# Output and feed-forward matmul chunks spread one by one over all even slots

## What is computed

```python
c_kv, c_q = h @ W_dkv, h @ W_dq                  # rank 128
k, v   = c_kv @ W_uk, c_kv @ W_uv                # 16 heads, 48 and 64 wide
q      = c_q @ W_uq ;  q_rot, k_rot = rotary(c_q @ W_qr), rotary(h @ W_kr)   # 16 wide
attn   = softmax([q, q_rot] @ [k, k_rot].T / 8) @ v
x      = layernorm(h + attn @ W_o)
w      = int4_rounded(W_ffn)
out    = layernorm(x + x @ w + bias + (x @ a) @ b)
```

## Time and profile before

| | us |
|---|---|
| median of 3 runs | 2160.74 (2158.69 to 2166.31) |
| the profiled execution, device time | 2158.53 |
| its span, core 6 (slowest) | 2157.0 |
| spans of the other cores | 2140.2 to 2154.1 |
| ScalarE busy | 2016.5 (93%) |
| TensorE busy | 1938.3 (90%) |
| VectorE busy | 602.7 (28%) |

### The profile page before, as it was taken

How to read it: one execution, slowest core, us unless ns; L and a number is a source line. 1 busy time by engine, 2 the same in 40 slices (tenths; PEclk the granted TensorE clock), 3 DMA queues, 4 the chain that set the end, 5 groups by cost and what they waited for, 6 DMA issues and landing times.

```text
span 2157.0 us, 61016 instructions; the slowest of 8 cores (2140.2 to 2157.0 us)
## 1 busy us (share of the span) xinstructions
PE 1938.3 (90%) x22544; PEld 708.4 (33%) x22544; DVE 602.7 (28%) x1084; ACT 2016.5 (93%) x2177; POOL 256.6 (12%) x303
## 2 busy tenths in 40 slices
PE   5977888989999999998999999999999999999976
PEld 2422333333333333333333333333333333333323
DVE  2731411232223322222222322323222322322224
ACT  2689999989999999998999999999999999999973
POOL 2000000110011110110111100211111100211021
PEclk9999999999999999999999999999999999999998
DMA  9772300121122211221121211312121311323121
GB/s 166 164 148 80 107 23 27 51 92 43 36 83 67 87 45 53 71 71 69 41 93 50 99 36 36 103 54 81 45 92 48 102 31 41 102 85 118 41 70 39
DMA packets 78681, 155.69 MB, mean 72 GB/s; under 512 B 16192, under 2 KB 46912, under 8 KB 78400
## 3 DMA queue, kind: packets, MB, share of 16 engines
q1 hardware_dynamic: 64672, 106.86, 15.5%
q0 software_dynamic: 13728, 44.93, 8.7%
HBM read 109.75 MB, written 40.76 MB: 70 GB/s over the span
## 4 chain that ended last, share of the span: by engine, by line
ACT 69%; issue 16%; PE 6%; DMA 3%; DVE 2%; ACTq 2%; SPq 1%; POOL 0%; DVEq 0%; POOLq 0%
ACT Psb L1004 69%; ACTq L998 2%; DMA wbuf<-hG 1%; DMA rbc<-rec 1%; SPq L495 1%; PE PS L742 1%; PE PS L916 1%; PE PS L858 1%; PE PS L944 1%; DMA osb<-hG 1%; PE PS L729 1%; PE PS L879 1%; PE PS L774 1%; PE PS L769 1%; PE PS L754 1%
## 5 line engine op out<-in xcount | busy, mean ns | idle before, releaser
L1004 ACT ACTIVATE Psb<-PS 128x1024 bf16<-128x1024 f32 x2048 | 1933.9, 1025 | 34.8 <-PE PS L858 22.5
L858 PE MATMUL PS<-Qsb,Ksb 64*128 64x512 bf16 x4096 | 804.0, 387 | 149.4 <-ACT Psb L1004 138.5
L879 PE MATMUL PS<-Psb,Vsb 128*32 128x512 bf16 x8192 | 634.1, 386 | 0.5 <-ACT Psb L1004 0.5
L858 PEld LDWEIGHTS PS<-Qsb,Ksb 64*128 64x128 bf16 x4096 | 212.9, 93 | 702.5 <-issue 696.4
L889 PE MATMUL PS<-Psb,ones_sb 128*32 128x256 bf16 x8192 | 404.1, 274 | 3.5 <-issue 3.5
L889 PEld LDWEIGHTS PS<-Psb,ones_sb 128*32 128x32 bf16 x8192 | 221.7, 97 | 224.2 <-issue 8.1
L1154 DVE TENSOR_TENSOR X<-PS,X 128x512 f32<-128x512 f32 x112 | 77.5, 692 | 625.5 <-PE PS L835 330.0
L879 PEld LDWEIGHTS PS<-Psb,Vsb 128*32 128x32 bf16 x8192 | 127.9, 94 | 236.5 <-issue 236.5
L831 PE MATMUL PS<-wbuf,osb 128*128 128x512 bf16 x448 | 135.6, 384 | 0.0
L802 PE MATMUL PS<-wbuf,osb 128*128 128x512 bf16 x448 | 135.6, 384 | 0.0
L1126 DVE COPY rec<-PS 128x256 f32<-128x256 f32 x64 | 27.1, 423 | 344.9 <-PE PS L889 344.9
(11 more groups left out here) (111 smaller groups left out, 690.8 us busy)
## 6 DMA issues: line engine op xcount, KB each, us to landing
wbuf<-wo_p POOLq DMA_DIRECT2D x32, 512.0 KB, 7.0
rbc<-rec SPq DMA_DIRECT2D x512, 32.0 KB, 1.8
X<-h SPq DMA_DIRECT2D x28, 512.0 KB, 3.9
x_scr<-X SPq DMA_DIRECT2D x28, 512.0 KB, 2.6
X<-x_scr SPq DMA_DIRECT2D x28, 512.0 KB, 3.4
wbuf<-wf_p POOLq DMA_DIRECT2D x28, 512.0 KB, 6.9
out<-X SPq DMA_DIRECT2D x28, 512.0 KB, 2.6
X<-W_ffn SPq DMA_DIRECT2D x16, 512.0 KB, 4.4
```

Of the source, the lines that this page charges most:

```text
L858: m = pe.matmul(PS[:, b0 + 512 * hh:b0 + 512 * (hh + 1)], Ksb[rows, k0:k0 + 128], Qsb[rows, 512 * p:512 * (p + 1)], tile_position=(64 * hh ...
L879: pe.matmul(PS[32 * j:32 * (j + 1), b0:b0 + 512], Vsb[:, v0:v0 + 32], Psb[:, p0 + 512 * (j // 2):p0 + 512 * (j // 2 + 1)], start=first and ...
L1004: act.activation(Psb[:, 1024 * (g % 4):1024 * (g % 4 + 1)], PS[:, 1024 * (g % 2):1024 * (g % 2 + 1)], AF.Exp, scale=0.125).then_inc(sem["e ...
```

## The change

`o` steps become 8 of one chunk and `f` steps 9 (the ninth is the low-rank matmul). The planner gives each `o` chunk 1.4 slots of its time and each `f` chunk 1.47, so an even slot holds one or two chunks of one group; the first chunk of a group begins a slot of its own, and every other step takes one even slot and moves the planner's time by 2. Waits and counts stay tied to the same matmuls. In tiles 1 to 6 the places become: `o` in slots 8 to 104; `qr` at 106 and 108; `qp` 0 to 2 at 112, 114 and 118; `tr` 3 at 116; `z` and `f` in slots 122 to 232 (`z` at 122, 150, 178, 206); `qp` 3 to 6 at 234, 236, 238 and 240. Of the even slots of such a tile 38 then have two chunks (18 `o`, 20 `f`), 60 have one (28 `o`, 32 `f`), and 12 are empty. The end of the last output group stays at slot 104 (chunk 7 alone), the end of the last feed-forward group moves from 244 to 232 (chunks 7 and 8), and with it GpSimd's load of the output weights.

```diff
-                    for i in range(4):
-                        seq.append((8, ("o", qt, sub, half, i)))
+                    for c in range(8):
+                        seq.append((8, ("o", qt, sub, half, c)))
...
-                    for i in range(5):
-                        seq.append((122, ("f", qt, sub, half, i)))
+                    for c in range(9):
+                        seq.append((122, ("f", qt, sub, half, c)))
...
         when = {}
-        t = 0.0
+        t, last = 0.0, -2
         for lo, st in seq:
             t = max(t, lo)
-            when[st] = 2 * int(t / 2 + 0.5)
-            at(T, when[st], st)
-            t += 2.8
+            if st[0] in ("o", "f"):
+
+                slot = max(last if st[-1] else last + 2, 2 * int(t / 2 + 0.5))
+                t += 1.4 if st[0] == "o" else 1.47
+            else:
+                slot = max(last + 2, 2 * int(t / 2 + 0.5))
+                t = slot + 2
+            when[st] = last = slot
+            at(T, slot, st)
...
-            for ph, kind, i in ((1, "o", 3), (2, "f", 4)):
+            for ph, kind, i in ((1, "o", 7), (2, "f", 8)):
...
-                at(T, when["o", qt, 3, 1, i] + 0.1, ("wf", qt, i))
-                at(T, when["f", qt, 3, 1, i] + 0.1, ("wo", qt, i))
+                at(T, when["o", qt, 3, 1, 2 * i + 1] + 0.1, ("wf", qt, i))
+                at(T, when["f", qt, 3, 1, 2 * i + 1] + 0.1, ("wo", qt, i))
```

TensorE's part, for `o` (that for `f` alike):

```diff
-                    sub, half, c2 = st[2:]
-                    if c2 == 0:
+                    sub, half, c = st[2:]
+                    if c == 0:
                         pe.wait_ge(sem["ev_misc"], misc_of(st))
-                    for c in (2 * c2, 2 * c2 + 1):
-                        if sub == 0 and half == 0:
...
-                        m = pe.matmul(bank(7), osb_tok(qt, sub, c),
...
+                    m = pe.matmul(bank(7), osb_tok(qt, sub, c),
...
-                    if c2 == 3:
+                    if c == 7:
                         m.then_inc(sem["mm_misc"], 1)
```

More of the change, by code:

```diff
@@ L361, in build_program @@
         for st in bg_at[g]:
-            if st[0] in ("qr", "qp", "tr", "z") or (st[0], st[-1]) in (("o", 3), ("f", 4)):
+            if st[0] in ("qr", "qp", "tr", "z") or (st[0], st[-1]) in (("o", 7), ("f", 8)):
                 misc_no[st] = n_misc
@@ L366, in misc_of @@
     def misc_of(st):
-        last = {"o": 3, "f": 4}
+        last = {"o": 7, "f": 8}
         return misc_no[st[:4] + (last[st[0]],)] if st[0] in last else misc_no[st]
@@ L669, in tail_step @@
                     else:
-                        gp.wait_ge(sem["mm_misc"], misc_no["f", qt, 3, 1, 4] + 1)
+                        gp.wait_ge(sem["mm_misc"], misc_no["f", qt, 3, 1, 8] + 1)
                     gp.dma_start(out=wbuf[:, 2048 * c:2048 * (c + 1)],
@@ L675, in tail_step @@
                     gp.wait_ge(sem["st_wf"], 128)
-                    gp.wait_ge(sem["mm_misc"], misc_no["o", qt, 3, 1, 3] + 1)
+                    gp.wait_ge(sem["mm_misc"], misc_no["o", qt, 3, 1, 7] + 1)
                     gp.dma_start(out=wbuf[:, 2048 * c:2048 * (c + 1)],
@@ L793, in tail_step @@
                 if st[0] == "o":
-                    sub, half, c2 = st[2:]
-                    if c2 == 0:
+                    sub, half, c = st[2:]
+                    if c == 0:
                         pe.wait_ge(sem["ev_misc"], misc_of(st))
-                    for c in (2 * c2, 2 * c2 + 1):
-                        if sub == 0 and half == 0:
-                            pe.wait_ge(sem["nrm_done"], NP * qt + c + 1)
-                            if c % 2 == 0:
-                                pe.wait_ge(ld_wo[c2], 16 * (qt + 1))
-                        m = pe.matmul(bank(7), osb_tok(qt, sub, c),
-                                      wbuf[:, 1024 * c + 512 * half:1024 * c + 512 * (half + 1)],
-                                      start=(c == 0), stop=(c == 7))
-                    if c2 == 3:
+                    if sub == 0 and half == 0:
+                        pe.wait_ge(sem["nrm_done"], NP * qt + c + 1)
+                        if c % 2 == 0:
+                            pe.wait_ge(ld_wo[c // 2], 16 * (qt + 1))
+                    m = pe.matmul(bank(7), osb_tok(qt, sub, c),
+                                  wbuf[:, 1024 * c + 512 * half:1024 * c + 512 * (half + 1)],
+                                  start=(c == 0), stop=(c == 7))
+                    if c == 7:
                         m.then_inc(sem["mm_misc"], 1)
@@ L824, in tail_step @@
                 if st[0] == "f":
-                    sub, half, c2 = st[2:]
-                    if c2 == 0:
+                    sub, half, c = st[2:]
+                    if c == 0:
                         pe.wait_ge(sem["ev_misc"], misc_of(st))
-                    if sub == 0 and half == 0 and c2 < 4:
-                        pe.wait_ge(ld_wf[c2], 16 * (qt + 1))
-                    for c in range(2 * c2, min(8, 2 * c2 + 2)):
+                    if sub == 0 and half == 0 and c < 8 and c % 2 == 0:
+                        pe.wait_ge(ld_wf[c // 2], 16 * (qt + 1))
+                    if c < 8:
                         pe.matmul(bank(7), osb_tok(qt, sub, c),
@@ L833, in tail_step @@
                                   start=(c == 0), stop=False)
-                    if c2 == 4:
+                    else:
                         pe.matmul(bank(7), zb_sb[:, :], bpad_sb[:, 512 * half:512 * (half + 1)],
@@ L1134, in ep_step @@
                     if qt >= 2 and p == 0:
-                        dve.wait_ge(sem["mm_misc"], misc_no["f", qt - 2, 3, 1, 4] + 1)
+                        dve.wait_ge(sem["mm_misc"], misc_no["f", qt - 2, 3, 1, 8] + 1)
                     dve.tensor_tensor(osb_pair(qt, p), bank(4 + P % 2), rbc[:, :], op=ALU.mult
@@ L1147, in tail_step @@
             def tail_step(st):
-                if (st[0], st[-1]) in (("o", 3), ("f", 4)):
+                if (st[0], st[-1]) in (("o", 7), ("f", 8)):
                     qt, sub, half = st[1:4]
```

## The result

The changed kernel takes 2178.77 us (median of 4 runs, 2178.54 to 2180.61), the kernel before 2160.23 (4 runs, 2158.69 to 2166.31): a ratio of 1.0078 with a 95% interval of 1.0056 to 1.0100, so it is slower, by 17 us. The median lies 0.8 above the upper end of the predicted range, 2178; the ratio times the 2160.74 that the prediction started from gives 2177.6, just inside it. The side and the two mechanisms are those forecast.

A forecast was written before the change was run, and what follows sets the result against it. ScalarE's exponentials on the slowest core were taken to bound the kernel. 2158.5 - 11 + 13 + 6 = 2166.5 us for a profiled execution, plus 2.2 for the runs' median, gave 2168 us, range 2148 to 2178 (forecast's own 2160 to 2175).

The forecast's parts named there:

- the two mechanisms: Weight loads meeting the ends of broadcasts at head pairs 2 and 6, making multiplies late: +6 and +13 us.
- What bounds the kernel: Whole kernel: ScalarE works 93% of 2157.0 us, nearly all on 2048 exponentials; the slowest core sets the time.
- Part 1: Output and feed-forward chunks: fewer heavy even slots save 1.6 us per tile, -11 us over seven tiles (-15 to -9).
- a cadence of 0.940: Sign for the chunk saving: exponentials among chunks come every 0.940 us instead of 0.951.
- Rival C: Added single-chunk visits on TensorE are not hidden and cost 21 us: 2171, up to 2182 us; chance 0.07.
- Part 2: Slots 96 and 104: pair 2's broadcast moves some 0.2 us closer to the feed-forward-weight load; +6 us, tiles 1 to 6.
- The announced sign: Slots 96 to 120 in tiles 4 to 6 take 24.4 us instead of 23.4, showing the pair 2 loss.
- Part 3: Slots 232 to 240: output-weight load meets pair 6's broadcast, its late multiply delays query chunks; +13 us (0 to 18).
- threshold of 3.1 us: Pair 6's multiply may start up to 3.1 us after the output-weight load starts; later delays TensorE's slot 238.
- Part 4: Slot 204: a feed-forward group ends where VectorE's multiply of pair 5 stands ahead of its addition; half a microsecond in all.
- rival D: Pair 2's shortened broadcast-to-load distance costs its upper bound in half the tiles: 15 us, not 6; 2177 to 2185; chance 0.08.
- Rivals A and B: A (0.25): pair 6's multiply in time, pair 2 unmoved, 2149.5 us; B (0.25): only pair 6 pays, 2162.5 us.

The follow-up runs named there:

- e7: Changed kernel, output-weight load held until head pair 6's multiply, one chunk moved from slot 96 to 94 and chunk 6 from 102 to 104: 0.9953 of the kernel before.
- e1: Changed kernel with the output-weight load held back until VectorE's multiply of head pair 6 is done: 1.0001 of the kernel before.
- e9: Changed kernel, output-weight load held until head pair 6's multiply, one output chunk moved from slot 96 to 94; second timing: 1.0001 of the kernel before.
- e5: Changed kernel with only query chunks 3 to 6 moved back, to slots 244 to 250, both weight loads unchanged: 0.9992 of the kernel before.
- e3: Changed kernel with output-weight and feed-forward-weight loads held back until the multiplies of head pairs 6 and 2 respectively: 0.9906 of the kernel before.
- e4: Kernel before with only the feed-forward-weight load held back until head pair 2's multiply is done: 0.9950 of the unedited kernel before.

## Why the prediction was right or wrong

**What bounds the kernel**: right. Wherever time was lost, the exponentials of line 1009 started late; in the kernel after they idle 27.2 us more than before, on slowest cores that differ by 22.1.

**Part 1, the chunks, -11 us**: right. It measured 0.9950 - 0.9906, 9.5 us, and 1 - 0.9953, 10.2 us, for e7, although e7 still stalls 3.1 more than the kernel before (17.7 + 1.7 against 14.1 + 2.2). So the pattern itself is worth 10 to 13; tile 7 says 1.7 x 7 = 12. Announced was a cadence of 0.940; it came to 0.942 beside the output chunks and 0.946 beside the feed-forward chunks. That the added visits are hidden holds too: single-chunk steps take 1.78 and 1.94, 3.72 together. The Trainium skill, TensorEngine Tiling (Array Packing), Key Properties, has TensorE drain at each change of the tiling mode. Paid in full at every added visit, by the price worked out from the rows, that would be 21 us; the trace does not agree as far as the time goes, since a single step ends before the next exponential does. Rival C is out.

**Part 2, slot 96 and slot 104, +6 us**: right in its mechanism, too small by four tenths. The shift of the broadcast was forecast as 0.12 to 0.18 and came to 0.18; the load came only 0.04 earlier, not 0.1. From e1 and e9 to e7 it measured 1.0001 - 0.9953 = 0.0048, 10.4 us. The term that was mis-sized is "I take 1 for each of tiles 1 to 6, nearer the quiet tiles": 6 us in the sum, 10.4 measured by the ratios, known to some 7, and 8 by the stalls of e1 and e7. Tiles 4 to 6 were quiet because the last issue stood 0.16 (odd cores) or 0.06 (even cores) ahead of the load. The earlier trace rows hold two points of that curve, 2.1 on core 7 and 3.5 on core 6, and I called it steep; a shift of 0.2 along it leads to 4.9 and 5.3, which is 2.5 per tile on an odd core and 2.0 on an even one, twice what I took. Tiles 1 to 3, which I had as lost already, lost more as well: their stall is 5.2 to 5.8 instead of 2.8 to 4.2. An instruction packet is beside all 24 of these meetings in both kernels, but the last issue is late (8.8 or more after slot 96) in 6 of them before and in 15 after, so part of this loss may not be the shift's. The announced sign, 24.4 for slots 96 to 120 in tiles 4 to 6, came out on the dear side: 26.8 on core 4 and 24.3 on core 5 in tile 4, and 26.2, 26.2 and 24.9 on the mean of the cores.

**Part 3, the feed-forward's end, +13 us**: right in its mechanism and nearly in size, 1.0078 - 1.0001, or 16.6 us, within its ends of 0 and 18. e1 and e5 show both halves of the chain. The threshold of 3.1 us held: where the multiply starts 2.1 after the load the stall is 0.2 to 0.3. Beyond it, in the 16 meetings in which the granted clock stays at its full level, the stall is that distance less 2.9, to a hundredth (3.5 gives 0.6, 4.8 gives 1.9). In 24 others the clock falls, and the stall is 1.1 to 2.3 more: 8.1 gives 7.5. These additions make 4.7 of the 20.1 us, so the 17.9 that pair 6 gained is 13 and the clock, as the prediction's middle and upper end had it. What I had wrong is which tiles pay. In tiles 5 and 6 the broadcast goes out at its earliest and the stall is 0.5 as forecast; tiles 1 to 4 pay 5.2, 4.0, 4.8 and 5.1, more evenly than I scaled them (tile 4 was to be one of the cheap ones). There the broadcast's issues end 0.3 to 1.5 later than in tiles 5 and 6 on most cores; on cores 4 and 6 they don't in tiles 1 to 3, and the stall is 1.1 to 4.6 all the same. Both go with the instruction packets, which the prediction did not have: that its sum was nearly right owes something to luck, as core 6's tile 1 stood for tiles 1 to 3, and tile 4 was counted cheap.

**Part 4, at most 0.5**: not tested by itself. e3 has the same group end at slot 204 and runs its tiles 1.4 faster than e4, which leaves little room for a loss there.

**The sum.** By the ratios of e7, e1 and the change, -10.2 + 10.4 + 16.6 = 16.8 us; that they add up is by construction, what the runs give is the split. I had -11 + 6 + 13 = 8, and 2168 us (2166.5 + 2.2 is 2168.7); 2178.8 is 10 above that and outside the forecast's own range of 2160 to 2175, by the two terms that were too small. Part 2 lies halfway between my 6 and the 15 of rival D, part 3 near its upper end, and the time is in the range that D gave. Rivals A and B are out: broadcasts do not land in time, and the small shift at pair 2 matters.

**Not settled.** In tiles 1 to 3 the last broadcast issue comes 8.8 to 9.8 after its slot instead of 8.2 to 8.5, in the changed kernel in 15 of 24 cases at pair 2 and 17 of 24 at pair 6; in tiles 5 and 6 never. In e3, where both loads of a core are held back, it is so in 12 of 24 at pair 2 and 19 of 24 at pair 6, so the load beside it doesn't cause it. In tiles 1 to 7 of the 11 profiles no broadcast takes over 4.4 us from first to last issue without an instruction packet beside it, but no run moved these packets. How a packet on one DMA engine keeps SyncE at an issue for a microsecond and more isn't shown, nor why it does so in some cases and not in others.

## What to carry to other kernels

When work on one queue is moved, list for every DMA it triggers what other transfer is in flight within the next microsecond, and who stands behind that one's consumer: a small transfer on a critical chain should be ordered ahead of a large load by a wait, not by luck of timing. Here such a wait for each load costs nothing that shows and turns a change that loses 0.8% into one that wins 0.9% (and the waiting load of the feed-forward weights is worth 0.5% in the kernel before, with no other edit: e4). And a margin read from a trace as 0.1 us is no margin: ask what happens on its other side before estimating a slope from it. Where the same transfer is late in some tiles and on time in others, look for `instruction` packets beside it before you scale one tile's stall to the next.

## What was not expected of the hardware

- A shift of 0.16 us in the order of two DMA issues, on two different engines' queues, decides up to 3 us of landing (1.9 against 3.6 to 4.9 on the odd cores of e9) and some 10 us of the kernel. The even cores' SyncE issues stand 0.1 after the odd ones' (8.30 against 8.20) in every kernel here, which puts them behind the edge in the kernel before; the odd cores pay as much once theirs are moved there too (e9).
- The program's own instruction packets, 8 or 16 KB on one of the 16 DMA engines, go with a broadcast issue that takes up to 2.9 us instead of 0.6. Without one, the eight issues take at most 4.4 us from first to last in every broadcast of tiles 1 to 7, in all 11 profiles.
- A stall costs more than its wait. Over the whole span the cores spend 61 to 102 us each with TensorE's clock granted at its lower level of 1.2 GHz in the kernel after, 30 to 61 before. At pair 6 of the kernel after it fell in 24 of 48 meetings and added 1.1 to 1.3 us to the stall in 13 of them, 1.5 to 2.3 in 11; the matmuls behind a long wait run 0.61 instead of 0.39 meanwhile, and the windows of slots 96 to 120 in tiles 1 to 3 show a mean of 0.83.
- Holding a 2 MB load back by over 3 us (in tiles 4 to 6 it starts 11.8 after slot 96 in e3, 8.32 in the changed kernel) costs the chunks that use its weights nothing that shows: tile 4 of e3 takes 241.9.
